# One kernel of full attention and two local-attention layers: step orders rearranged, first weights loaded a phase earlier

## The chip, the cores and the metric

The kernel runs on one core of a Trainium2 chip. The metric is device time in microseconds (us) of one execution. The times of before are three runs; the profile is one further execution of the same program.

## The reference, cut to what matters

The input `x` is 16 sequences of 512 rows and 256 columns, float32. It is layer-normed once (`xn`), and two branches are computed from `xn`: full attention with 16 heads, and two "layers" of local attention with a gated feed-forward.

```python
xn = layernorm(x)
x  = x + attn(xn, w_qkv, w_out) + layers(xn)
def layer(x):                                   # twice, 8 heads of 64, window 128
    h = shift_token(x); q, k, v = split(h @ wqkv)
    q, k = rotary_xpos(l2norm(q) * qs, l2norm(k) * ksc)
    x = x + local_attention(q * 8, k, v) @ wo   # each block of 128 sees itself and the block before
    h = layernorm(shift_token(x)) * lg + lb
    a, g = split(h @ w1 + b1)
    return x + (a * gelu(g)) @ w2 + b2
```

## The kernel before, in words

The program is two phases, one after the other, each a block of five instruction streams: PE (matmuls and transposes), ACT, DVE, POOL and SP (which issues every DMA). A block ends when all five are through and the last stores have landed; only then does the next begin.

**Full attention** (`full_attention_phase`) walks over the 16 sequences. Its last section, "end", is three rounds: B of sequence 14, B of sequence 15, and the tail T of sequence 15. POOL's last step in it comes some 110 us before its end.

**Layers** (`layers_phase`) first loads and converts weights: SP issues loads of `wqkv`, the two rotation tables, the two scales and `wo`; ACT makes the float16 high parts (`wq_h`, `wo_h`), DVE the low parts (`wq_l`, `wo_l`) and scales the tables; POOL makes identity matrices and masks. SP issues the first of these loads after `const_done`, which DVE's clears raise, and after adding 1 to each of the phase's 55 semaphores (`start_credits`). Behind these six loads it issues the first load of the input, `f_xs`, on whose transposes (step A.XT) everything waits.

The two layers are layer 0 and layer 1. Each walks over the 16 sequences in rounds. A round works on four sequences at once: stream A projects queries and keys of sequence i, C does attention of i-1, D the output projection and N the layer norm of i-2, F the feed-forward of i-3. Thirteen rounds of a layer are one loop body; the first three ("first", "second", "third") and the last ("tail") are written out with some streams missing. The dictionary `order` lists, for each engine, the steps of one round in the order in which the engine issues them; an engine never passes a step that waits. The steps that matter here:

- A.XT transposes the input; A.QK,t projects 128 rows to queries and keys: PE L1026, squares on ACT L1212, on DVE L1350 to L1359, and on POOL the add L1540 (`bt_used`). A.RN is a chain of 12 small DVE operations (L1385, L245 to L250) which ends with `rn_ready` (L1387). A.NM,t scales by it on POOL (L1545, 128x1024), A.HI,t makes high parts on ACT (L1222, L1223), A.SQ,t and A.SH,t the low parts on POOL (L1550, L1535).
- C.V projects values (PE L1026, ACT, DVE L1368). C.L1,hp computes scores to find the row maximum (DVE L1392), C.LM hands the maxima on, C.L2,hp computes the scores of two heads again (PE) and their exponentials (ACT L1245), C.PH,hp the float16 high parts (ACT L1253), C.PL,hp the low parts (DVE L1374, two operations of 128x896, both inputs in SBUF), C.PV,hp multiplies by the values (PE L1113 to L1115) and divides (DVE L1403, L1405).
- D.WO,c is the output projection (PE L1133, DVE L1424). N.LN takes the statistics (DVE L1442), N.LR the root (POOL L1530, L1518 to L1523), N.LA applies them (DVE L1456, eight operations, both source and target in SBUF), N.XH transposes the result (PE L1008, ACT L1262, DVE L1462), N.LS adds a bias (POOL L1562).
- F.W1,f and F.W2 are the feed-forward: F.W1,f on PE L1162, ACT L1268, DVE L1472; F.H1,f on ACT (L1274, L1276) and POOL (L1556); F.ZB adds the full attention's result on DVE (L1433, layer 1 only); F.W2,0 to 2 on PE L1133, with an eviction after part 2 (DVE L1483). On DVE and SP the parts 0 and 1 of F.W2 issue nothing.

The results on PE go to four PSUM slots of 128x1024. Which step gets which slot is not written down: `PsumPlan` walks PE's order once and gives each step the slot used longest ago (a slot used by A.QK counts as used 2.5 steps later). A PE step waits until its slot's former user is drained. Each section starts the walk with the slots in the same turn, so in a loop C.V,0 always takes slot p0, C.V,1 p1, C.V,2 p2 and C.V,3 p3.

Of the kernel before, what the change touches and what calls it, by code (L numbers as in the profile page):

```python
# [1684 lines left out]
```

## Time and profile before

| what | value |
|---|---|
| median of 3 runs | 3927.06 us (3926.61 to 3927.91) |
| time of the profiled execution | 3927.97 us |
| its span, first to last instruction | 3926.1 us |
| mean granted TensorE clock | 0.953 |
| busy: PE, PEld, DVE, ACT, POOL | 3360.0, 1960.8, 2846.7, 2352.7, 1511.6 us |

The full attention fills the span up to 1155.1 us; the layers' first transposes start at 1172.25 us. From there on the rounds follow each other at about 81 us each. The page's busy share is an average over both phases; the waits of one round tell more.

### The profile page before, as it was taken

The numbers are of one execution on the slowest core, as the hardware profiler recorded it, in microseconds if no ns is written. First come the engines' busy times: TensorE is split into PE (matmuls) and PEld (weight loads), VectorE is DVE, ScalarE is ACT, GpSimd is POOL, SyncE is SP. The second block draws the span as 40 slices with busy tenths as digits, with TensorE's granted clock in tenths as the row PEclk, the third lists the DMA queues.
The fourth block names the chain that finished last, engine by engine and source line by source line (L and its number), as shares of the span: only waits on it lengthen the run. The fifth ranks groups of instructions, "written<-read, shape, count | busy, mean of one in ns | idle before, by whom it ended". The sixth has DMA issues, their size and how long they took to land.

```text
span 3926.1 us, 77200 instructions
## 1 busy us (share of the span) xinstructions
PE 3360.0 (86%) x29600; PEld 1960.8 (50%) x29600; DVE 2846.7 (73%) x4121; ACT 2352.7 (60%) x2813; POOL 1511.6 (39%) x1171
## 2 busy tenths in 40 slices
PE   2888888888855799998999989878999899998998
...
GB/s 56 49 61 54 60 53 60 52 60 52 51 50 39 15 20 19 27 19 29 19 20 26 25 23 36 30 44 24 25 32 24 35 29 24 32 29 36 24 27 30
DMA packets 149008, 139.11 MB, mean 35 GB/s; under 512 B 11132, under 2 KB 147376, under 8 KB 148912
## 3 DMA queue, kind: packets, MB, share of 16 engines
...
## 4 chain that ended last, share of the span: by engine, by line
PE 35%; DVE 15%; ACT 11%; issue 7%; POOL 1%; DMA 1%; SPq 0%; DVEq 0%; ACTq 0%; POOLq 0%
PE f_p L1026 13%; PE f_p L1162 7%; DVE f_Ph L1374 6%; PE f_p L1133 5%; PE f_p L1052 3%; PE f_p L1043 3%; ACT f_Ph L1253 2%; ACT f_Pl L1245 2%; DVE f_xh L1456 2%; PE f_p L1059 2%; ACT f_hT L1274 1%; DVE f_rt L248 1%; ACT f_gates L1268 1%; DVE f_xT_l L1343 1%; PE f_p L1008 1%
## 5 line engine op out<-in xcount | busy, mean ns | idle before, releaser
L654 DVE TENSOR_REDUCE m_negm<-m_p 128x2 f16<-128x1024 f32 x512 | 608.7, 1222 | 169.2 <-PE m_p L473 167.5
L576 ACT ACTIVATE m_Pr<-m_p 128x1024 f32<-128x1024 f32 x512 | 500.4, 1020 | 164.0 <-PE m_p L492 159.6
L1374 DVE TENSOR_TENSOR f_Ph<-f_Pl,f_Ph 128x896 f16<-128x896 f32 x256 | 377.0, 1514 | 213.3 <-ACT f_Ph L1253 213.3
L1540 POOL TENSOR_TENSOR f_u<-f_u,f_bt 128x1024 f32<-128x1024 f32 x128 | 301.8, 2358 | 465.6 <-DVE f_bt L1359 465.6
L1556 POOL TENSOR_TENSOR f_hT<-f_gates,f_hT 128x512 f16<-128x512 f32 x192 | 234.2, 1223 | 587.9 <-ACT f_gates L1276 587.6
L1268 ACT ACTIVATE f_gates<-f_p,f_bias 128x512 f32<-128x512 f32 x192 | 131.4, 684 | 469.0 <-PE f_p L1162 469.0
L501 PE MATMUL m_o<-m_Pr,m_vm 128*32 128x512 f32 x2048 | 341.6, 646 | 13.0 <-ACT m_Pr L576 13.0
L1026 PE MATMUL f_p<-f_wq_h,f_xT_h 128*128 128x512 f16 x768 | 307.0, 400 | 26.1 <-DVE f_xhT_l L1462 12.7
L1545 POOL TENSOR_TENSOR f_u<-f_u,f_rn 128x1024 f32<-128x1024 f32 x128 | 289.1, 2258 | 74.3 <-DVE f_mark_v L1387 74.3
L1392 DVE TENSOR_REDUCE f_negm<-f_p 128x4 bf16<-128x1024 f32 x256 | 300.8, 1222 | 17.0 <-PE f_p L1059 16.6
L1026 PE MATMUL f_p<-f_wq_l,f_xT_h 128*128 128x512 f16 x768 | 305.3, 398 | 0.0
L1026 PE MATMUL f_p<-f_wq_h,f_xT_l 128*128 128x512 f16 x768 | 303.1, 395 | 0.0
L1550 POOL TENSOR_TENSOR f_qst<-f_u,f_qst 128x512 f16<-128x512 f32 x128 | 179.6, 1403 | 270.8 <-ACT f_khh L1223 270.8
L1245 ACT ACTIVATE f_Pl<-f_p 128x896 f32<-128x896 f32 x256 | 227.4, 915 | 91.9 <-PE f_p L1097 56.9
L1113 PE MATMUL f_p<-f_vl,f_Ph 128*128 128x65 f16 x1792 | 187.4, 197 | 95.4 <-DVE f_Ph L1374 80.9
L1133 PE MATMUL f_p<-f_w_h,f_hT 128*128 128x256 f16 x1536 | 262.8, 273 | 1.6 <-POOL f_hT L1556 1.4
L473 PE MATMUL m_p<-m_KT,m_QT 48*128 48x512 f16 x1024 | 192.4, 399 | 80.7 <-DMA m_KT<-m_lo 31.4
L1472 DVE SCALAR_TENSOR_TENSOR f_gates<-f_p,f_bias,f_gates 128x512 f32<-128x512 f32 x192 | 141.6, 750 | 161.2 <-ACT f_gates L1268 158.4
L1162 PE MATMUL f_p<-f_xhT_h,f_w_h 128*128 128x512 f16 x640 | 245.0, 383 | 2.4 <-DVE f_mark_h L1464 2.4
L492 PE MATMUL m_p<-m_QT,m_KT 49*128 49x512 f16 x1024 | 191.9, 390 | 61.7 <-DVE m_negm L654 35.8
L1162 PE MATMUL f_p<-f_xhT_h,f_w_l 128*128 128x512 f16 x640 | 244.0, 381 | 0.0
L1162 PE MATMUL f_p<-f_xhT_l,f_w_h 128*128 128x512 f16 x640 | 243.8, 381 | 0.0
...
## 6 DMA issues: line engine op xcount, KB each, us to landing
f_xs<-out SPq DMA_DIRECT2D x32, 512.0 KB, 4.4
f_xr<-out SPq DMA_DIRECT2D x32, 512.0 KB, 5.0
out<-f_xb SPq DMA_DIRECT2D x32, 512.0 KB, 3.0
m_xin<-in_L_attn_x SPq DMA_DIRECT2D x16, 512.0 KB, 4.1
out<-m_xn SPq DMA_DIRECT2D x16, 512.0 KB, 3.0
m_QT<-m_hi SPq DMA_DIRECT2D x128, 64.0 KB
m_KT<-m_hi SPq DMA_DIRECT2D x128, 64.0 KB
m_xr<-in_L_attn_x SPq DMA_DIRECT2D x16, 512.0 KB, 4.7
```

The costliest lines, as they stand in the source:

```text
L501: mm = pe.matmul(psum[w.slot("MV", g)][j * VW:(j + 1) * VW, :], vm[I.par][:, kt, g * HG + j, :], Pr[kt % 2][:, j, :], start=(kt == 0), sto ...
L576: act.activation(Pr[kt % 2][:, 2 * u:2 * u + 2, :].rearrange("p h t -> p (h t)"), psum[w.slot("M2", g, kt, u)][:, :], ACT.Exp).then_inc(*w ...
L654: dve.tensor_reduce(negm[:, t, pr // 2, :, pr % 2], psum[w.slot("M1", h, u)][:, :].rearrange("p (a k) -> p a k", a=2), AX.X, ALU.max, nega ...
L1026: mm = pe.matmul(psum[w.slot(key, t)][:, i * INNER:(i + 1) * INNER], a_[:, c, at], b_[:, c, n0:n0 + INNER], start=(c == 0 and k == 0), sto ...
L1133: mm = pe.matmul(psum[w.slot(key)][:, t * D:(t + 1) * D], a_[:, c, t * P:(t + 1) * P], b_[:, c, :], start=(c == 0 and k == 0 and t % 2 == ...
L1162: mm = pe.matmul(psum[w.slot("W1", f)][0:rows(f), g * T:(g + 1) * T], a_[:, c, hidden(g, f)], b_[:, c, :], start=(c == 0 and k == 0), stop ...
L1245: act.activation(Pl[h % 2][:], psum[w.slot("L2", h)][:, 0:NK], ACT.Exp, scale=1 / KBOOST)\
L1374: dve.tensor_tensor(Pp[h % 4][:, 1, :], Pl[h % 2][:], Pp[h % 4][:, 0, :], ALU.subtract).then_inc(*p_lo_ready.up(I))
L1392: dve.tensor_reduce(negm[:, :, h], psum[w.slot("L1", h)][:, :].rearrange("p (n k) -> p n k", n=NT), AX.X, ALU.max, negate=True).then_inc(* ...
L1540: pool.tensor_tensor(u[t][:], u[t][:], bt[:], ALU.add).then_inc(*bt_used.up(I))
L1545: pool.tensor_tensor(u[t][:].rearrange("p (h d) -> p h d", d=DH), u[t][:].rearrange("p (h d) -> p h d", d=DH), rn[:, t, :].unsqueeze(2).to ...
L1556: pool.tensor_tensor(hT_l[0:n, f, :], hp_[f % 3][0:n, :], hT_h[0:n, f, :], ALU.subtract).then_inc(*hl_ready.up(I))
```

## The change

Two things. First, a new class `First` holds the tensors that both phases now share: the layers' weight tensors for queries, keys, values and output, tables, masks, identities and their staging space. Its `load` issues the first layer's six loads on SP in the full attention's last section, in front of the last tail (step "PW"). Its `constants` and `prepare` run on POOL after POOL's last step of the full attention: identities and masks, then, once all six loads have landed, the conversion of both weights and the scaling of the tables, all with POOL's `tensor_tensor`. In the layers phase ACT and DVE skip these steps for layer 0, and SP raises their semaphores by hand (eight `sem_inc`).

Second, the dictionary `order` of the layers is changed on all five engines.

```diff
+        def load(self, sp, q_scale, k_scale):      # class First
+        start(self.st_q, self.wqkv[0].rearrange("(c p) n -> p c n", p=P))
+        start(self.cos_t[:], ...)   # sin_t, qk_scale 0, qk_scale 1
+        start(self.st_o, self.wo[0].rearrange("(c p) n -> p c n", p=P))
+    def prepare(self, pool):
+        done = 0
+        pool.wait_ge(self.loaded, 6 * 16)
+        for src, high, low in ((self.st_q, self.wq_h, self.wq_l), (self.st_o, self.wo_h, self.wo_l)):
+            def factor(n):
+                return self.factors[:, n:n + 1].unsqueeze(2).to_broadcast([P, src.shape[1], src.shape[2]])
+            for dst, a, b, op in ((src, src, factor(4), ALU.mult), (high[:], src, factor(5), ALU.mult), (low[:], src, high[:], ALU.subtract)):
+                pool.tensor_tensor(dst, a, b, op).then_inc(self.steps, 1)
+                done += 1
+                pool.wait_ge(self.steps, done)
+        for i in range(2):
+            pool.tensor_tensor(cos_t[:, :, i, :], cos_t[:, :, i, :], qk_scale[:, i:i + 1, :]..., ALU.mult)
+            for h in range(2):
+                pool.tensor_tensor(sin_t[:, :, i, half], sin_t[:, :, i, half], ..., ALU.mult)
...
                               woven(order, B=a("B_15", 1, lambda i: last), T=a("T_14", 0, lambda i: last - 1)),
+                              {engine: [("PW", a("weights", 0, lambda i: 0))] for engine in ENGINES},
                               woven(order, T=a("T_15", 1, lambda i: last)))),
...
             w.run({"LN": ln, "PQ": pq, "SP": sp_})
+            first.constants(pool)
+            first.prepare(pool)
...
-        "PE": """... A.QK,3 D.WO,0 C.L1,0 D.WO,1 D.WO,2 D.WO,3 C.L1,1 ...
+        "PE": """... A.QK,3 C.L1,0 D.WO,0 D.WO,1 D.WO,2 D.WO,3 C.L1,1 ...
-        "ACT": """... F.H1,1 F.W1,3 C.LM F.H1,2 F.W1,4 F.H1,3 F.W1,5 F.H1,4 F.H1,5 C.L2,0 C.PH,0 ...
+        "ACT": """... F.H1,1 F.W1,3 F.H1,2 C.LM F.W1,4 F.H1,3 F.W1,5 F.H1,4 C.L2,0 F.H1,5 C.PH,0 ...
-        "DVE": """C.V,0 C.V,1 C.V,2 C.V,3 A.XT D.OT,0 D.OT,1 A.QK,0 A.QK,1 A.QK,2 A.QK,3 D.WO,0 D.WO,1 D.WO,2 C.L1,0 D.WO,3 C.L1,1
-               F.W1,0 C.L1,2 F.W1,1 C.L1,3 C.LM F.W1,2 A.RN F.W1,3 F.W1,4 F.W1,5 F.ZB N.LN F.W2,0 C.PL,0 C.PL,1 F.W2,1 F.W2,2 N.LA
-               C.PL,2 C.PV,0 C.PL,3 C.PV,1 N.XH C.PV,2 C.PV,3""",
-        "POOL": """A.QK,0 A.QK,1 A.QK,2 A.QK,3 F.H1,0 F.H1,1 F.H1,2 F.H1,3 F.H1,4 F.H1,5 A.NM,0 N.LR A.SQ,0 A.SH,0 A.NM,1 A.SQ,1 A.SH,1
-               A.NM,2 A.SQ,2 A.SH,2 A.NM,3 A.SQ,3 A.SH,3 N.LS""",
-        "SP": """A.XT N.LX C.XR F.W2,0 F.W2,1 F.W2,2 N.XH""",
+        "DVE": """C.V,0 C.V,1 C.V,2 C.V,3 A.XT D.OT,0 D.OT,1 A.QK,0 A.QK,1 A.QK,2 C.L1,0 A.QK,3 D.WO,0 D.WO,1 D.WO,2 D.WO,3 C.L1,1
+               F.W1,0 C.L1,2 F.W1,1 C.L1,3 F.W1,2 C.LM F.W1,3 N.LN F.W1,4 A.RN F.W1,5 F.ZB F.W2,0 F.W2,1 C.PL,0 C.PL,1 F.W2,2 N.LA
+               C.PL,2 C.PV,0 C.PV,1 C.PL,3 N.XH C.PV,2 C.PV,3""",
+        "POOL": """A.QK,0 A.QK,1 A.QK,2 F.H1,0 F.H1,1 A.QK,3 F.H1,2 F.H1,3 A.NM,0 F.H1,4 F.H1,5 N.LR A.SQ,0 A.SH,0 A.NM,1 A.SQ,1 A.SH,1
+               A.NM,2 A.SQ,2 A.SH,2 A.NM,3 N.LS A.SQ,3 A.SH,3""",
+        "SP": """A.XT F.W2,0 N.LX C.XR F.W2,1 F.W2,2 N.XH""",
...
             def wq(I):                             # SP; ws(I) likewise with wo_loaded
+                if layer == 0:
+                    for signal, n in ((wq_loaded, 16), (tables_loaded, 64), (w_hi, 1), (w_lo, 1), (tables_done, 1)):
+                        sp.sem_inc(*signal.up(I, n))
+                    return
-                sp.wait_ge(const_done, N_CONST)
```

## Rows read from the trace of the kernel before

**Rows 1.** Windows view: us, busy time by engine, granted clock, DMA share, GB/s.
```profile
1155.10:1172.20 17.10, 0.00 (x0) 0.00 (x0) 6.89 (x19) 3.82 (x2) 8.10 (x21) 0.50 0.54 188
3225.50:3306.30 80.80, 73.72 (x735) 49.52 (x734) 62.27 (x98) 53.24 (x66) 40.46 (x30) 1.00 0.10 29
```

**Rows 2.** Timeline, engine PE: first transpose of A.XT, rounds 3 and 15 of layer 1.
```profile
2737.84 0.32 PE L1008 MATMUL f_p<-f_identf,f_xs 128*128 128x128 f32 x1
...
3711.28 0.33 PE L1008 MATMUL f_p<-f_identf,f_xs 128*128 128x128 f32 x1
```

**Rows 3.** Waits of PE in one round, 3225.5 to 3306.3: total, times, longest.
```profile
PE f_p L1113 <- DVE f_Ph L1374: 2.6, 1, 2.6
...
PE f_p L1008 <- DVE f_on L1405: 0.9, 1, 0.9
PE f_p L1026 <- DVE f_xhT_l L1462: 0.6, 1, 0.6
PE f_p L1085 <- DVE f_gates L1472: 0.5, 1, 0.5
```

**Rows 4.** Timeline of the same round, engine DVE: start, length, operation, wait before.
```profile
3264.15 0.19 DVE L1385 TENSOR_SCALAR f_ss<-f_ss 128x64 f32<-128x64 f32 x1
...
3269.07 0.06 DVE L1387 MEMSET f_mark_v<- 1x1 f32 x1
...
3283.01 3.96 DVE L1374 TENSOR_TENSOR f_Ph<-f_Pl,f_Ph 128x896 f16<-128x896 f32 x2 [2.82 <-ACT f_Ph L1253]
...
3288.15 0.34 DVE L1456 TENSOR_SCALAR f_xh<-f_x,f_mv,f_rstd 128x128 f32<-128x128 f32 x1
...
3290.19 2.10 DVE L1374 TENSOR_TENSOR f_Ph<-f_Pl,f_Ph 128x896 f16<-128x896 f32 x2
...
3294.11 3.96 DVE L1374 TENSOR_TENSOR f_Ph<-f_Pl,f_Ph 128x896 f16<-128x896 f32 x2 [0.98 <-ACT f_Ph L1253]
...
3298.96 1.22 DVE L1462 TENSOR_TENSOR f_xhT_l<-f_p,f_xhT_h 128x1024 f16<-128x1024 f32 x1
...
3301.18 0.69 DVE L1405 TENSOR_TENSOR f_on<-f_p,f_rden 128x512 f32<-128x512 f32 x1
```

**Rows 5.** Timeline of the same round, engine ACT.
```profile
3282.03 1.79 ACT L1253 ACTIVATE f_Ph<-f_Pl 128x896 f16<-128x896 f32 x2
```

**Rows 6.** Timeline of the same round, engine POOL.
```profile
3275.83 1.89 POOL L1545 TENSOR_TENSOR f_u<-f_u,f_rn 128x1024 f32<-128x1024 f32 x1
...
3281.04 1.16 POOL L1550 TENSOR_TENSOR f_qst<-f_u,f_qst 128x512 f16<-128x512 f32 x1
...
3283.27 2.76 POOL L1545 TENSOR_TENSOR f_u<-f_u,f_rn 128x1024 f32<-128x1024 f32 x1
```

**Rows 7.** Timeline of layer 0's third round, engine DVE.
```profile
1356.02 3.05 DVE L1374 TENSOR_TENSOR f_Ph<-f_Pl,f_Ph 128x896 f16<-128x896 f32 x2 [2.14 <-ACT f_Ph L1253]
...
1360.09 1.94 DVE L1456 TENSOR_SCALAR f_xh<-f_x1s,f_mv,f_rstd 128x128 f32<-128x128 f32 x1
```

**Rows 8.** Timeline of layer 0's third round, engine POOL.
```profile
1353.01 1.74 POOL L1518 TENSOR_TENSOR f_rstd<-f_var,f_factors 128x4 f32<-128x4 f32 x1
...
1356.10 2.02 POOL L1550 TENSOR_TENSOR f_qst<-f_u,f_qst 128x512 f16<-128x512 f32 x1
```

**Rows 9.** Timeline between the phases, engine POOL.
```profile
1155.14 0.20 POOL L1494 MEMSET f_ident<- 128x128 f16 x1 [111.36 <-POOLq L377]
```

**Rows 10.** Timeline between the phases, the DMA queue of SP.
```profile
1125.71 0.39 SPq L753 DMA_DIRECT2D m_xr<-in_L_attn_x  x1
...
1158.34 0.38 SPq L1573 DMA_DIRECT2D f_u<-in_L_ffn_wqkv  x1
...
1161.12 0.87 SPq L1573 DMA_DIRECT2D f_Ph<-in_L_ffn_wo  x1
```

**Rows 11.** DMA view, 1120 to 1180: KB each, us from issue to landing.
```profile
f_Ph<-in_L_ffn_wo SPq DMA_DIRECT2D x1, 512.0 KB, 9.6
```

**Rows 12.** The page, DMA issues over the whole span.
```profile
f_xs<-out SPq DMA_DIRECT2D x32, 512.0 KB, 4.4
```

More of the change, by code:

```diff
@@ L298, in full_attention_phase @@
+def full_attention_phase(nc, counts, x, w_qkv, w_out, out, attn_res, first, q_scale, k_scale):
     B, T, D = x.shape
@@ L767, in mp @@
                 sp.dma_start(res_v[I.b], res[:]).then_inc(*res_stored.up(I, 16))
-            w.run({"LX": lx, "XR": xr_, "LS": ls, "ST": stack, "MM": mmax, "MP": mp})
+            w.run({"LX": lx, "XR": xr_, "LS": ls, "ST": stack, "MM": mmax, "MP": mp, "PW": lambda I: first.load(sp, q_scale, k_scale)})
             end = Inst("after", 0, None)
@@ L775, in full_attention_phase, with layers_phase @@
     return ph.measured()
-def layers_phase(nc, counts, wqkv, q_scale, k_scale, wo, ln_g, ln_b, w1, b1, w2, b2, out, attn_res):
+def layers_phase(nc, counts, wqkv, q_scale, k_scale, wo, ln_g, ln_b, w1, b1, w2, b2, out, attn_res, first):
     B, T, D = out.shape
@@ L884, in layers_phase @@
         psum = {s: ctx.enter_context(nc.psum_tensor("f_" + s, [P, 1024], F32)) for s in pools["pair"]}
-        wq_h, wq_l = sb("wq_h", [P, NC, 3 * INNER], F16), sb("wq_l", [P, NC, 3 * INNER], F16)
-        wo_h, wo_l = sb("wo_h", [P, NP_, D], F16), sb("wo_l", [P, NP_, D], F16)
+        wq_h, wq_l, wo_h, wo_l, U, Pall = first.wq_h, first.wq_l, first.wo_h, first.wo_l, first.U, first.Pall
+        cos_t, sin_t, qk_scale, factors = first.cos_t, first.sin_t, first.qk_scale, first.factors
+        ident, identb, identf, masks, mask0, sel = first.ident, first.identb, first.identf, first.masks, first.mask0, first.sel
         w1_h, w1_l = sb("w1_h", [P, NC, 2 * HID], F16), sb("w1_l", [P, NC, 2 * HID], F16)
@@ L949, in layers_phase @@
         sp_held = ctx.enter_context(nc.semaphore("f_sp_held"))
[L950 to L951 removed]
+        const_done = ctx.enter_context(nc.semaphore("f_const_done"))
+        N_CONST = 7
         out_v = out.rearrange("b (t p) d -> b p t d", p=P)
@@ L1588, in ws @@
             def ws(I):
-                if I.b > 0:
-                    hold(on_ready.at(all_of_layer(I.b), 0))
+                if I.b == 0:
+                    for signal, n in ((wo_loaded, 16), (w_hi, 1), (w_lo, 1)):
+                        sp.sem_inc(*signal.up(I, n))
+                    return
+                hold(on_ready.at(all_of_layer(I.b), 0))
                 load(I, wo_loaded, st_o, wo[I.b].rearrange("(c p) n -> p c n", p=P))
@@ L1648, in program @@
     attn_res = nc.dram_tensor("attn_res", x.shape, F32, kind="Internal").ap()
-    found = full_attention_phase(nc, counts, x, w_qkv, w_out, out, attn_res)
-    return found | layers_phase(nc, counts, wqkv, q_scale, k_scale, wo, ln_g, ln_b, w1, b1, w2, b2, out, attn_res)
+    with ExitStack() as ctx:
+        first = First(nc, ctx, out, wqkv, wo)
+        found = full_attention_phase(nc, counts, x, w_qkv, w_out, out, attn_res, first, q_scale, k_scale)
+        return found | layers_phase(nc, counts, wqkv, q_scale, k_scale, wo, ln_g, ln_b, w1, b1, w2, b2, out, attn_res, first)
 _INS = ["L0_attn_x", "L0_attn_w_qkv", "L0_attn_w_out", "L0_ffn_wqkv", "L0_ffn_q_scale", "L0_ffn_k_scale", "L0_ffn_wo",
```

118 lines of the change are left out of this document (75 added, 43 removed).

## The prediction

> **What bounds the kernel now.** I read the windows view first: in the 17.1 us between the phases PE does nothing, and in a round of the layers it is busy 73.7 of 80.8 us [rows 1]. The reader is to see two kinds of gain: the gap between the phases, and the 7 us of PE's gaps in each of 26 loop rounds. A.XT comes every 81.1 us ((3711.28 - 2737.84) / 12) [rows 2], so a change of 0.3 us in the round is a change of 8 us, or 0.2% of the kernel; that is also what I take to be indistinguishable from no change.
>
> The waits of PE in a round say where the gaps are [rows 3]: 2.6 us in front of C.PV,3 for DVE's low parts, 0.9 in front of N.XH's transposes, 0.6 in front of C.V,0, 0.5 in front of C.L2,0; a further 1.5 in front of C.L2,3 is a wait for F.W2's slot. All but the 0.5 lie in the last 28 us of the round. There the chain is not PE's: it goes exponentials, C.PH (ACT), C.PL (DVE), C.PV. The timelines of DVE and POOL show what stretches it. A pair of C.PL operations takes 2.10 us alone, but 3.96 in C.PL,1 and C.PL,3 [rows 4], and the A.NM that POOL starts 0.26 us into C.PL,1 takes 2.76 instead of 1.89 [rows 6]. So one waits until the other's operation is over: A.NM for the first of the pair, the second of the pair for A.NM. What matters in that stretch is who comes when, not how much each engine has to do.
>
> **The preload.** Removed between the phases: the wait for the loads and their conversion, up to A.XT. What stays ahead of A.XT is SP's credits, the load of `f_xs` and its landing. The credits alone put SP's first DMA 3.2 us behind the start of the phase (1158.34 - 1155.14) [rows 9, 10]; eight more at 3.2 / 55 add 0.5; landing takes 4.4 [rows 12]. A.XT thus starts 8.3 us into the phase instead of 17.1: -8.8.
>
> Added: the phase now begins only when POOL is through. The loads go out where the tail's `m_xr` load did, at 1125.7 [rows 10]. On the old path the last of them went out 2.8 us after the first and landed 9.6 later [rows 10, 11]; so they land at 1138.1. POOL's identities and masks lie in its 111.36 us of idleness [rows 9] and cost nothing. The conversion: 128x1024 float32 with one operand repeated from one number takes POOL 1.89 us, two operands of 128x512 1.16 [rows 6]. Weights for queries: two multiplications of 3072 columns (5.7 each) and one subtraction (6.9); for the output a third of that; tables six small ones, 2.5 together. Sum 18.3 + 6.1 + 2.5 = 27, end 1165.2. The phase before ended at 1155.1, so +10.1. Net +1.3 us. If every operand cost the two-operand rate (2.3 per 1024 columns), 3 us more; if the loads land 3 us earlier, with no `f_xs` behind them, 3 less: -2 to +4.5.
>
> The Trainium skill (GPSIMD Engine Reference, section 3.1) gives 4497 ns for a two-input float32 operation of 2048 columns, 2.2 us per 1024, without a cheaper rate for a repeated operand; the row with its 1.89 is below it. By the page the conversion would take 29 us and the preload +3.5.
>
> The tail's `m_xr` load moves behind six issues and 7 us of traffic, to about 1140; its reader runs at 1150, so nothing waits. On the path it would cost its lateness.
>
> **Moves at no cost.** C.L1,0 in front of D.WO,0 on PE finds both slots free (those of A.ST,3, which ACT drains in time); DVE then does C.L1,0 in front of A.QK,3, which comes 2.5 us later and still before the eviction of D.WO; 0.3 us of lateness ends in DVE's idle time ahead of F.W1,0. POOL's A.QK,3 behind F.H1,1 fills idle time; its readers are A.NM,3 and nobody sooner. N.LS in front of A.SQ,3 delays A.ST,3 of the next round, 13 us away. The parts of F.W2 moved on SP and DVE issue nothing. Without these covers each is worth under 1 us a round.
>
> **Gains in the round.** A.RN leaves the place in front of F.W1,3's eviction, which frees C.L2,0's slot: -0.5, the whole wait [rows 3]. C.L2,0's exponentials go ahead of F.H1,5. C.PV,1 goes ahead of C.PL,3 into DVE's idle 0.98 [rows 4], so N.XH's eviction no longer stands behind it: -0.9. These would make the round 1.4 us shorter if C.PL,3 ended as early as before.
>
> **Losses.** First, A.RN. It ran from 3264.15 to 3269.07 [rows 4], with two stalls. Behind F.W1,4 it starts at 3269.6 and, with one stall of 1, ends at 3273.5. POOL meanwhile has nothing (F.H1,4 now stands behind A.NM,0). Then A.NM,0, F.H1,4 and F.H1,5 take 1.9 + 1.16 + 1.16 and end at 3277.8, just when A.NM,0, then the last of the three, ended before (3275.83 + 1.89) [rows 6]. But C.PL,0 is ready at 3276.9, 1.2 earlier than before, and queues ahead of N.LR. Layer 0's third round has this order already: N.LR's second operation takes 1.74 us there, and A.SQ,0 starts only at the moment of C.PL,1 [rows 7, 8]. In the new round N.LR so ends at 3282.2 instead of 3281.0, C.PL,1 is ready at 3282.4 (C.PH's first operation, 3282.03 before [rows 5], half a us earlier), and A.SQ,0 and A.SH,0 push in: C.PL,1 ends at 3285.4 to 3286.5 (3286.97 before), but A.NM,1 has not run yet. It starts at 3286.5 where it had ended at 3286.0, just in front of N.LA. N.LA's operations take 0.34 us and met nobody [rows 4]; in the third round one of them waits 1.94 behind A.NM,1 [rows 7]. So N.LA ends at 3290.4, as before, in spite of the early start; C.PL,2 follows, A.SQ,1, A.SH,1 and A.NM,2 fall between C.PL,2 and C.PL,3, and C.PL,3 ends at 3298.5 against 3298.07: +0.4 where -0.9 was there to be had. In layer 1, F.ZB (128x1024, 1.2 us) waits for A.NM,0 and keeps F.H1,4 waiting; POOL is 1.2 to 1.5 us later, and C.PL,3 ends at 3299.2: +1.1.
>
> Of this the rule is the Trainium skill's (SBUF, State Buffer, section on the two separate sides): a DVE operation with two SBUF inputs or in a two-port mode and a GpSimd operation exclude each other for the whole operation, and whoever starts first goes first. The stretched rows agree. By the rule every C.PL and N.LA operation moved into POOL's busy stretch pays; it speaks against this change.
>
> Second, the slots. Walked, the new PE order gives C.V,0's slot p0 to C.PV,3 (before: to N.XH). C.V,0 now waits for DVE's last C.PV eviction, 2.9 us after C.PL,3 (3298.96 to 3301.87) [rows 4], where it waited only for N.XH's. The order on DVE being N.XH, C.PV,2, C.PV,3, the next A.XT comes 8.45 us after C.PL,3 ends; before it came 8.23 after in layer 1 and 7.75 in layer 0, where no load of `f_xs` is waited for. That is +0.2 and +0.7, and it already holds the gain from moving C.PV,1.
>
> Sum: layer 0 13 x (0.4 + 0.7) = 14, layer 1 13 x (1.1 + 0.2) = 17. The third rounds get A.RN behind N.LN: +1.5 each; the two tails, with no stream A, keep the gains: -1.5 each. With the preload +1.3 the profiled execution's 3927.97 becomes 3960; it lies 0.9 above the median, so 3959 to 3960.
>
> **Rivals.**
> 1. As computed: +0.5 to +1.9 a round, 3940 to 3980. For it speaks that the third round shows each collision. 0.46.
> 2. Faster: A.NM,1 gets in ahead of N.LA and C.PL,3's two operations run back to back, which takes 2.10 instead of 3.96 [rows 4]. C.PV,1 ahead of C.PL,3 makes this possible: if C.PL,3 starts after the second C.PH has ended, its second operation queues ahead of A.NM,2. Then C.PL,3 ends at 3296.2, -1.9, with the slots -1.4 a round, -37 in all: 3890. It decides whether A.NM,2 is issued before or after C.PL,3's second operation is ready, a matter of 0.5 us. Against it: N.LR's and A.SQ,0's lateness. 0.23.
> 3. Even: only one collision goes away, and slots and preload take it back: 3920 to 3935. 0.17.
> 4. F.H1,5 comes later than the 3280 at which F.W2,2 needs it, and PE's chain slips as well: +2.5 a round, 3992. 0.14.
> That the preload fails to take effect is no rival of its own: it is worth under 5 us either way.
>
> Range: 3888 to 3985; the likeliest case alone 3940 to 3980. Faster 0.24, same 0.19, slower 0.57.
>
> **What would show it.** A.XT first at 1173 to 1175, POOL busy up to 1165. Loop rounds of 82.2 (layer 0) and 82.4 (layer 1). No wait of PE ahead of C.L2,0; C.V,0 waiting for L1405; N.LA's L1456 with operations of 1 to 2 us in every round; A.NM,1 starting behind 3286 in a round that starts at 3225.5. If L1456 stays at 0.34 and C.PL,3 lasts 2.1, the second case holds. If C.V,0 still waits for L1462, I walked the slots wrongly.

## The result, and the profile after

The changed kernel takes 3987.9 us (median of 4 runs, 3982.1 to 3990.2) against 3926.8 for the kernel before: ratio 1.0154, 95% interval 1.0138 to 1.0170, 61 us slower. The prediction was 3960 with a range to 3985: the direction was right, the loss of 61 us nearly twice the 33 computed, and 3 us beyond the range's end. The profiled execution took 3986.68 us with a span of 3984.9, 58.8 more than before. PE was busy 3396.1 us against 3360.0 for the same 29600 matmuls, and its mean granted clock was 0.939 against 0.953. That is a first hint: part of the loss is that the same work ran more slowly.

Cut at the starts of A.XT, the 58.8 us are: -4.3 up to the first A.XT; +0.4 in layer 0's three written-out rounds; +10.7 in twelve loop rounds (81.07 to 81.96 each); +1.6 in the stretch between the layers (layer 0's last loop round and its tail); +7.5 in layer 1's three written-out rounds; +28.5 in twelve rounds of layer 1 (81.12 to 83.49); +14.4 from there to the end (the last loop round, the tail and the last stores).

Timeline of the changed kernel, engine PE: the A.XT of rounds 3 and 15 of layer 1 (the answer to [rows 2]). Line numbers of `layers_phase` have shifted: by 77 on PE, by 80 to 84 on ACT and DVE, by 63 on POOL. In e1, e3 and e4 below they are 7 lower than in the changed kernel.
```profile
2753.77 0.31 PE L1085 MATMUL f_p<-w_identf,f_xs 128*128 128x128 f32 x1
...
3755.68 0.49 PE L1085 MATMUL f_p<-w_identf,f_xs 128*128 128x128 f32 x3
```
Windows view of the changed kernel: two consecutive rounds of layer 1, then the last 16 and 19 us of each (columns as in [rows 1]).
```profile
3257.00:3339.10 82.10, 74.74 (x736) 51.11 (x735) 63.32 (x97) 53.03 (x65) 42.64 (x29) 0.98 0.10 29
3339.10:3424.20 85.10, 78.38 (x735) 53.07 (x734) 64.73 (x99) 53.33 (x65) 45.28 (x32) 0.92 0.09 28
3323.00:3339.10 16.10, 10.49 (x121) 7.33 (x118) 11.77 (x19) 9.35 (x13) 14.13 (x8) 0.89 0.21 65
3405.00:3424.20 19.20, 14.38 (x128) 9.51 (x124) 12.82 (x21) 9.88 (x13) 15.44 (x9) 0.64 0.16 55
```
The two rounds differ by 3.0 us. In their last stretch the granted clock is 0.89 in the one and 0.64 in the other, while C.PL,3 ends at 74.1 us of the round in both. Most rounds of layer 1 alternate between these two kinds. So a round has to be read in two parts: up to the end of C.PL,3, which the chain of DVE, ACT and POOL sets, and from there to the next A.XT, where the last evictions and PE's own matmuls set the pace, at whatever clock PE is granted.

Waits of PE in the first of these rounds (the answer to [rows 3]): total, times, longest.
```profile
PE f_p L1085 <- DVE f_on L1489: 3.1, 1, 3.1
PE f_p L1103 <- DVE f_on L1489: 1.3, 1, 1.3
PE f_p L1190 <- DVE w_Ph L1458: 1.2, 1, 1.2
PE f_p L1210 <- POOL f_hT L1619: 1.1, 1, 1.1
PE f_p L1200 <- DVE f_xT_l L1427: 0.4, 1, 0.4
PE f_p L1210 <- DVE f_gates L1556: 0.3, 1, 0.3
```
N.XH (L1085) waits 3.1 us for the eviction of C.PV,0, whose slot it gets; C.V,0 (L1103) waits 1.3 for that of C.PV,3; C.PV,3 (L1190) waits 1.2 for C.PL,3; F.W2,2 waits 1.1 for F.H1. The wait ahead of C.L2,0 that the change removes is indeed gone.

Timeline of that round, engine DVE (the answer to [rows 4]).
```profile
3300.79 0.29 DVE L1526 BATCH_NORM_STATS2 f_stats<-f_x 128x6 f32<-128x128 f32 x1 [2.46 <-DMA f_x1s<-f_x]
...
3303.42 0.18 DVE L1469 TENSOR_SCALAR f_ss<-f_ss 128x64 f32<-128x64 f32 x1
...
3306.46 0.06 DVE L1471 MEMSET f_mark_v<- 1x1 f32 x1
...
3309.91 3.60 DVE L1458 TENSOR_TENSOR w_Ph<-f_Pl,w_Ph 128x896 f16<-128x896 f32 x2 [0.33 <-ACT w_Ph L1333]
...
3315.33 2.11 DVE L1458 TENSOR_TENSOR w_Ph<-f_Pl,w_Ph 128x896 f16<-128x896 f32 x2 [1.82 <-ACT w_Ph L1333]
...
3318.61 1.20 DVE L1540 TENSOR_SCALAR f_xh<-f_x,f_mv,f_rstd 128x128 f32<-128x128 f32 x1
3319.73 1.94 DVE L1540 TENSOR_SCALAR f_xh<-f_x1s,f_mv,f_rstd 128x128 f32<-128x128 f32 x1
...
3323.14 2.08 DVE L1458 TENSOR_TENSOR w_Ph<-f_Pl,w_Ph 128x896 f16<-128x896 f32 x2
...
3327.04 3.97 DVE L1458 TENSOR_TENSOR w_Ph<-f_Pl,w_Ph 128x896 f16<-128x896 f32 x2
```
Same round, engine POOL (the answer to [rows 6]).
```profile
3306.60 1.90 POOL L1608 TENSOR_TENSOR w_u<-w_u,f_rn 128x1024 f32<-128x1024 f32 x1 [3.83 <-DVE f_mark_v L1471]
3308.46 4.10 POOL L1619 TENSOR_TENSOR f_hT<-f_gates,f_hT 128x512 f16<-128x512 f32 x2
...
3318.58 1.15 POOL L1598 TENSOR_TENSOR f_klt<-w_u,f_khh 128x512 f16<-128x512 f32 x1
3319.69 1.90 POOL L1608 TENSOR_TENSOR w_u<-w_u,f_rn 128x1024 f32<-128x1024 f32 x1
```
The first row of DVE is what the prediction left out: N.LN, moved ahead of F.W1,4, waits 2.46 us for the transfer of shifted rows `f_x1s`, and A.RN (L1469 to L1471) with `rn_ready` stands behind it. Relative to its round's start A.RN ends at 49.5 us, not at 48.0 as computed and not at 43.6 as before. Further down most collisions are where they were computed: N.LA's first two operations take 1.20 behind A.SH,0 and 1.94 against A.NM,1, C.PL,1 its short 2.11, C.PL,3 still 3.97. Not computed was that F.H1,4 and 5 take 4.10 where they meet F.ZB and C.PL,0, and that C.PL,0 takes 3.60. C.PL,3 ends at 74.0 (72.6 before), 1.4 late; +1.1 was computed.

The preload: conversion on POOL, from landing to the last table.
```profile
1133.27 5.31 POOL L366 TENSOR_TENSOR w_u<-w_u,w_factors 128x3072 f32<-128x3072 f32 x1 [85.01 <-DMA w_Ph<-in_L_ffn_wo]
...
1158.42 0.86 POOL L375 TENSOR_TENSOR w_sin<-w_sin,w_qk_scale 128x128 f32<-128x128 f32 x2
```
It takes 26.0 us (27 computed). The first A.XT comes at 1168.0; in the other profiles of kernels with the preload, below, it comes anywhere from 1167.3 to 1174.2, so its -4.3 here is within the scatter of single executions. In e1's profile the loads land at 1138.0, where they were computed, and the first A.XT comes at 1172.9.

### The profile page after: what moved, and what is told of

Its sections match the earlier page's. It is cut to its first block, busy times and chain, and to the rows that moved or that the text cites. A ratio compares the mean times of both kernels' runs of the same rounds, so it can differ in the third digit from the quotient of the medians.

```text
span 3984.9 us, 77447 instructions
## 1 busy us (share of the span) xinstructions
PE 3396.1 (85%) x29600; PEld 2002.9 (50%) x29600; DVE 2847.3 (71%) x4115; ACT 2349.6 (59%) x2811; POOL 1596.6 (40%) x1185
## 4 chain that ended last, share of the span: by engine, by line
PE 22%; DVE 17%; DMA 11%; issue 9%; ACT 8%; POOL 2%; SPq 1%; DVEq 0%; POOLq 0%; ACTq 0%
PE f_p L1103 12%; DMA f_x1s<-f_x 11%; DVE w_Ph L1458 4%; PE f_p L1120 2%; DVE f_xh L1540 2%; ACT w_Ph L1333 2%; ACT f_Pl L1325 2%; DVE f_negm L1476 1%; PE f_p L1239 1%; PE f_p L1210 1%; DVE f_ss L1434 1%; PE f_p L1129 1%; DVE f_xT_l L1427 1%; ACT f_hT L1354 1%; DVE w_u L1437 1%
## 5 line engine op out<-in xcount | busy, mean ns | idle before, releaser
L1603 POOL TENSOR_TENSOR w_u<-w_u,f_bt 128x1024 f32<-128x1024 f32 x128 | 302.3, 2361 | 492.2 <-DVE f_bt L1443 492.2
L1619 POOL TENSOR_TENSOR f_hT<-f_gates,f_hT 128x512 f16<-128x512 f32 x192 | 250.7, 1312 | 595.4 <-ACT f_gates L1356 595.4
L1458 DVE TENSOR_TENSOR w_Ph<-f_Pl,w_Ph 128x896 f16<-128x896 f32 x256 | 364.3, 1462 | 120.1 <-ACT w_Ph L1333 119.0
L1103 PE MATMUL f_p<-w_wq_h,f_xT_h 128*128 128x512 f16 x768 | 306.7, 399 | 43.9 <-DVE f_on L1489 32.0
L1608 POOL TENSOR_TENSOR w_u<-w_u,f_rn 128x1024 f32<-128x1024 f32 x128 | 270.1, 2110 | 184.5 <-DVE f_mark_v L1471 184.5
L1476 DVE TENSOR_REDUCE f_negm<-f_p 128x4 bf16<-128x1024 f32 x256 | 301.3, 1224 | 28.8 <-PE f_p L1136 28.5
L1103 PE MATMUL f_p<-w_wq_l,f_xT_h 128*128 128x512 f16 x768 | 303.5, 395 | 0.0
L1103 PE MATMUL f_p<-w_wq_h,f_xT_l 128*128 128x512 f16 x768 | 302.2, 394 | 0.0
L1190 PE MATMUL f_p<-f_vl,w_Ph 128*128 128x65 f16 x1792 | 208.4, 206 | 64.9 <-DVE w_Ph L1458 45.2
L1613 POOL TENSOR_TENSOR f_qst<-w_u,f_qst 128x512 f16<-128x512 f32 x128 | 209.0, 1633 | 132.4 <-ACT f_khh L1303 132.4
```

The lines of the kernel that those rows point to most:

```text
L1103: mm = pe.matmul(psum[w.slot(key, t)][:, i * INNER:(i + 1) * INNER], a_[:, c, at], b_[:, c, n0:n0 + INNER], start=(c == 0 and k == 0), sto ...
L1458: dve.tensor_tensor(Pp[h % 4][:, 1, :], Pl[h % 2][:], Pp[h % 4][:, 0, :], ALU.subtract).then_inc(*p_lo_ready.up(I))
L1476: dve.tensor_reduce(negm[:, :, h], psum[w.slot("L1", h)][:, :].rearrange("p (n k) -> p n k", n=NT), AX.X, ALU.max, negate=True).then_inc(* ...
L1603: pool.tensor_tensor(u[t][:], u[t][:], bt[:], ALU.add).then_inc(*bt_used.up(I))
L1608: pool.tensor_tensor(u[t][:].rearrange("p (h d) -> p h d", d=DH), u[t][:].rearrange("p (h d) -> p h d", d=DH), rn[:, t, :].unsqueeze(2).to ...
L1619: pool.tensor_tensor(hT_l[0:n, f, :], hp_[f % 3][0:n, :], hT_h[0:n, f, :], ALU.subtract).then_inc(*hl_ready.up(I))
```

## The experiments

For each kernel two numbers were read from its trace, as means over twelve loop rounds of each layer: when C.PL,3 ends in its round (start and length of the last L1458 row), and how long it takes from there to the next A.XT. "Base" is the changed kernel with the five orders of before. Times are medians; the kernel before ran beside them at 3927.6 to 3928.4.

| kernel | us | C.PL,3 ends, layer 0 / 1 | then to A.XT, layer 0 / 1 |
|---|---|---|---|
| before | 3928 | 72.6 / 72.6 | 8.5 / 8.5 |
| changed | 3987.9 | 73.3 / 74.1 | 8.7 / 9.4 |
| e1 preload alone (base) | 3925.1 | 72.6 / 72.6 | 8.5 / 8.5 |
| e2 orders alone | 3970.9 | 72.6 / 73.5 | 9.3 / 9.1 |
| e3 changed, N.LN back | 3947.5 | 71.9 / 72.5 | 10.3 / 9.4 |
| e11 changed, N.LN and C.L1,0 back | 3901.5 | 72.0 / 72.6 | 8.0 / 8.0 |
| e13 changed, C.L1,0 back | 3954.3 | 73.2 / 74.0 | 8.1 / 7.9 |
| e14 base, C.L1,0 moved | 3996.4 | 72.6 / 72.6 | 11.0 / 11.1 |
| e6 e3, C.L1,0 back on PE alone | 3958.0 | 74.0 / 75.2 | 8.1 / 7.8 |
| e10 e3, C.PV,0 early | 3996.7 | 72.6 / 72.8 | 10.9 / 10.9 |
| e5 e3, A.RN back | 4039.9 | 74.7 / 74.6 | 10.8 / 10.7 |
| e12 e5, A.QK,3 back | 3964.8 | 72.6 / 72.6 | 10.1 / 10.1 |
| e4 changed, A.NM,0 back | 4062.1 | 75.3 / 75.3 | 10.1 / 10.4 |
| e8 base, C.L2,0 and A.RN moved | 3988.3 | 75.2 / 75.2 | 7.9 / 8.4 |
| e7 base, C.PV,1 early | 3910.2 | 72.6 / 72.6 | 8.0 / 8.0 |
| e9 e7, A.NM,1 held | 3878.2 | 71.4 / 71.5 | 7.9 / 7.9 |

**Halves of the change.** e1 keeps the preload and has all orders of before; e2 is the kernel before with the new orders.

> The changed kernel with all five orders of before: the preload alone. Theory: the preload costs what the account of the phase boundary gives (8.8 us of gap gone, some 10 us of POOL conversion added), so 3928 us against 3926.9. Rival: the 5.6 us by which the full attention was shorter in the profile of after come with the preload, then 3922. If the preload were part of the loss, it would be above 3935.

> The kernel before with the five new orders and no preload. Theory: the orders are the whole loss: 3983 to 3990 us. Rival: orders and preload interact (the weights of both phases lie elsewhere in SBUF), then under 3975.

e1: 3925.1, ratio 0.9991 (0.9982 to 1.0000): the preload is worth between nothing and 7 us, 3 by the medians. e2: 3970.9, ratio 1.0107 (1.0092 to 1.0123), under both figures of its theory and on its rival's side: the halves don't add up (+43 and -3 against +61). The loss is the orders', but they cost 63 us on top of the preload (3987.9 against e1's 3925.1) and 43 without it. The rows show where some of it comes from: the second of the two issues that fill `f_x1s` (the shifted rows that N.LN waits for) takes 11.4 us on SP's queue (median) in the kernel before and in e2, and 11.8 in e1 and in the changed kernel, and N.LN's wait in a loop round is 1.8 to 2.0 us in e2 and 2.4 to 2.7 in the changed kernel. Loop rounds of layer 1 with the short last stretch are 81.5 and 82.1. So the slower transfer goes with the preload, which puts tensors elsewhere, and not with the orders; why it does stays open.

**N.LN.**
```diff
-  DVE  ... C.LM F.W1,3 N.LN F.W1,4 A.RN F.W1,5 F.ZB F.W2,0 ...
+  DVE  ... C.LM F.W1,3 F.W1,4 A.RN F.W1,5 F.ZB N.LN F.W2,0 ...      # e3
```


> The changed kernel with one step of DVE moved: N.LN stands behind F.ZB again, as before, and not ahead of F.W1,4. Theory A: the step that fails in the prediction is N.LN's wait of 2.6 us for the DMA f_x1s, which delays A.RN, F.H1,4 and 5 and all behind; without it each of 26 rounds gets 1.5 to 2.5 us back: 3922 to 3950. Theory B (the prediction's own: A.RN's new place, the collisions behind it and the slots): N.LN is only a fraction, 0 to 0.5 us a round: 3973 to 3988.

3947.5, ratio 1.0049 (1.0036 to 1.0063): 40 us came back, inside theory A's range. C.PL,3 ends 1.5 us earlier in layer 1 and 1.3 in layer 0; A.RN ends at 48.0 instead of 49.5, just where the prediction had put it. But C.PL,3 now ends at 71.9 and 72.5, ahead of the kernel before, where the prediction without any wait had it at 73.0 and 73.7: the rest of its chain was 1.1 to 1.2 us too slow. In layer 0 of e3 N.LA's operations take 0.67 us at the most, not 1.94. Much of the written-out rounds' loss goes as well: layer 1's first round falls from 75.6 to 67.5 us (65.4 before), the stretch behind the last A.XT of the loop from 229.2 to 214.3. Yet the second part of the round grows, in layer 0 from 8.7 to 10.3 us. N.LN's wait is one cause, and there is another.

The transfer in the chain of the changed kernel's round (start, length, what) with a window of 10 us in it, then the wait for it in layer 1's first round, where N.LN comes early for want of other work, in the kernel before and in the changed one.
```profile
3284.76 16.00 DMA f_x1s<-f_x
```
```profile
3286.00:3296.00 10.00, 10.00 (x66) 5.12 (x65) 6.89 (x8) 4.22 (x7) 1.15 (x1) 1.00 0.08 19
```
```profile
DVE f_stats L1442 <- DMA f_x1s<-f_x: 2.5, 1, 2.5
```
```profile
DVE f_stats L1526 <- DMA f_x1s<-f_x: 8.6, 1, 8.6
```
`f_x1s` is half of x1's columns, each row moved one partition on, so the copy writes 127 partitions (254 KB) in a first issue and the rows that wrap around (1.5 KB) in a second. It lands 16.0 us after the second issue. While it is the only transfer, the DMA share is 0.08 of 16 engines, the time of little more than one, and 19 GB/s move; `f_xs`, twice the size, lands in 4.3 us. So the rows show a copy that is hardly spread over the engines; whether one that is spread would end N.LN's wait was not tried. In the chain of the whole changed kernel the transfer holds 11% of the span.

**The slots: C.L1,0.** By a walk over PE's order, moving C.L1,0 ahead of D.WO,0 gives C.V,0 the slot of C.PV,3. Three kernels put it back (e6 on PE alone), and one moves it alone.
```diff
   PE   ... A.QK,3 [C.L1,0] D.WO,0 [C.L1,0] D.WO,1 ...      # first place: change, second: before
   DVE  ... A.QK,2 [C.L1,0] A.QK,3 D.WO,0 D.WO,1 D.WO,2 [C.L1,0] D.WO,3 ...
   # e6:  e3, PE alone back      e11: e3, PE and DVE back
   # e13: changed kernel, both back      e14: base, both moved
```


> N.LN behind F.ZB as in the run before, and on PE C.L1,0 behind D.WO,0 again, which by the walk of the slots gives C.V,0 back the slot of N.XH. Theory (the prediction's slot step): 0.2 us a round in layer 1 and 0.7 in layer 0, so 8 to 14 us below N.LN alone (3947): 3933 to 3939. Rival: C.V,0's wait only moves to another step of the same stretch, since all evictions there stand behind C.PL,3: 3943 to 3950.

3958.0, ratio 1.0073 (1.0056 to 1.0090), slower than e3 by 11 us, which neither side expected. Waits of PE in a round of e6:
```profile
PE f_p L1085 <- DVE f_on L1489: 3.1, 1, 3.1
PE f_p L1129 <- DVE f_bt L1443: 1.9, 1, 1.9
```
With DVE still in the new order, C.L1 (L1129) waits 1.9 us in mid-round for A.QK,2's slot, and C.PL,3 comes 2.1 to 2.7 us later than in e3. Behind C.PL,3 the run does show what C.V,0's slot is worth: no wait of C.V,0 is left, and the second part of the round falls from 10.3 and 9.4 to 8.1 and 7.8 us.

> The changed kernel with N.LN behind F.ZB (3947), and C.L1,0 back on both engines: on PE behind D.WO,0, on DVE behind D.WO,2. In the run with PE's C.L1,0 alone back, PE waited 1.9 us for the drain of A.QK,2's slot. Theory: that wait is gone, and C.V,0 has N.XH's slot, which gives 0.3 us a round: 3932 to 3942. Rival: C.L1,0's place does not matter: 3944 to 3950.

3901.5, ratio 0.9931 (0.9914 to 0.9947): 46 us below e3 and faster than the kernel before. Three times the most that the theory gave. C.PL,3 ends where it does in e3; all of the gain lies behind it. The fastest kind of round of layer 0 in e11, then e3's slowest, cut 70 us after their starts (windows view; the means over layer 0 are 79.9 and 82.2).
```profile
1779.10:1849.10 70.00, 66.68 (x669) 45.99 (x667) 55.33 (x88) 48.21 (x58) 34.25 (x26) 1.00 0.09 26
1849.10:1858.78 9.68, 6.87 (x66) 3.53 (x67) 5.49 (x10) 4.42 (x7) 7.99 (x6) 1.00 0.00 0
```
```profile
1705.67:1775.67 70.00, 66.65 (x669) 46.03 (x667) 54.72 (x87) 48.20 (x58) 32.99 (x24) 1.00 0.09 26
1775.67:1789.39 13.72, 10.64 (x66) 5.51 (x67) 6.67 (x11) 4.91 (x7) 9.63 (x7) 0.63 0.00 0
```
The same 66 matmuls take PE 6.87 us in the one and 10.64 in the other. The granted clock is 1.00 (2.4 GHz) against 0.63, a mixture with the lower level of 1.2 GHz. In both rounds PE stood 1.3 us ahead of N.XH and 2.6 ahead of C.PV,3; in e3 it stood another 1.0 ahead of C.V,0, and the projections of C.V that follow ran at half clock, where nothing but PE sets the pace. The Trainium skill says that frequent short idle stretches between groups of matmuls make the clock swing between its two levels (TensorE: Matmul & The Clock Gate, the section on PSUM-queue cycling). These two rounds agree. Which of several rounds with the same waits is hit, the rows do not show.

> The changed kernel (3988) with C.L1,0 alone back, on PE behind D.WO,0 and on DVE behind D.WO,2; N.LN stays ahead of F.W1,4. Theory: C.V,0's wait for C.PV,3's eviction is a second gap near the end of the round, and with it PE's clock falls to half for longer; without it 1.0 to 1.8 us a round come back, beside N.LN's wait which stays: 3938 to 3962. Rival: the two share one cause, and with N.LN's wait in place C.L1,0 is worth little: 3975 to 3990.

> Preload and the five orders of before (3925), with C.L1,0 alone moved as in the change: on PE ahead of D.WO,0, on DVE ahead of A.QK,3. Theory: C.V,0 gets the slot of C.PV,3, whose eviction comes last, and PE's clock stays low longer: 1.2 to 2 us a round, 3955 to 3977. Rival: the prediction's slot step, 0.2 to 0.7 us a round: 3930 to 3940.

e13: 3954.3, ratio 1.0069 (1.0052 to 1.0086), 34 us back with N.LN's wait in place, as its theory has it. e14: 3996.4, ratio 1.0176 (1.0159 to 1.0193): this one move in the old orders costs 71 us over e1, more than the whole change, and more than its theory gave. Windows of a round of e14 and of one of e1, from 70 to 83 us behind their starts at 3185.24 and 3144.03, each followed by the timeline row of the first matmul of C.V,0.
```profile
3255.24:3268.24 13.00, 9.16 (x71) 5.04 (x68) 8.07 (x14) 5.30 (x8) 9.63 (x7) 0.74 0.24 81
```
```profile
3261.69 0.61 PE L1103 MATMUL f_p<-w_wq_h,f_xT_h 128*128 128x512 f16 x1 [1.25 <-DVE f_on L1489]
```
```profile
3214.03:3227.03 13.00, 9.79 (x87) 5.52 (x85) 8.81 (x15) 5.99 (x10) 9.63 (x7) 0.87 0.25 81
```
```profile
3218.77 0.61 PE L1096 MATMUL f_p<-w_wq_h,f_xT_h 128*128 128x512 f16 x1 [0.64 <-DVE f_xhT_l L1539]
```
C.V,0 starts at 76.45 in its round instead of 74.74: +1.7, the direct cost of the slot in the old DVE order. A loop round is 2.5 longer than in e1; the other 0.8 goes with the clock. In e1 it is 1.00 in rounds of 80.3 to 81.1 us and 0.98 in those of 80.6 to 81.6; in e14 it is 0.96 in every loop round, and no round is under 82.9.

**A.RN, A.QK,3 and the order on POOL.** e5 takes e3 and puts A.RN back ahead of F.W1,3; e12 takes e5 and puts POOL's A.QK,3 back behind A.QK,2; e4 takes the changed kernel and puts A.NM,0 behind F.H1,5; e8 takes base, puts A.RN behind F.W1,3 and, on ACT, C.L2,0 ahead of F.H1,5.

> The changed kernel with two steps of DVE back where they were: N.LN behind F.ZB, and A.RN ahead of F.W1,3. Theory: with N.LN alone back, rn_ready still comes 4.4 us later than before; with A.RN back too, A.NM,0 and F.H1,4 start earlier and only C.V,0's slot and the 3.1 us gap ahead of N.XH are left: 3925 to 3940. Rival: A.RN's place is indifferent once N.LN has gone, or its new place is even good (C.L2,0's slot comes free sooner): 3945 to 3955.

> The kernel of 4040 (N.LN and A.RN back on DVE) with POOL's A.QK,3 back behind A.QK,2. Theory: in the 4040 kernel A.QK,3 of 2.4 us on POOL ran into A.RN, one of whose operations took 2.3 us and two 1.1, and rn_ready came 2 us late; with A.QK,3 back this goes away: 3915 to 3935. Rival: the 4040 comes from F.H1,4 and F.H1,5 or the clock alone: above 4000.

e5: 4039.9, ratio 1.0284 (1.0267 to 1.0301), far above both figures. DVE and then POOL in a round of it:
```profile
3345.60 2.29 DVE L249 SCALAR_TENSOR_TENSOR f_rt<-f_rt,f_ss 128x64 f32<-128x64 f32 x1
```
```profile
3345.45 2.36 POOL L1603 TENSOR_TENSOR w_u<-w_u,f_bt 128x1024 f32<-128x1024 f32 x1
```
An operation of 0.23 us on DVE takes 2.29 because A.QK,3's addition on POOL has begun 0.15 us ahead of it; A.RN ends 2.0 us late, and F.W1,3's eviction behind it frees C.L2,0's slot 2.0 us later than before (PE stands 2.6 us there). e12 removes that: 3964.8, ratio 1.0098 (1.0081 to 1.0115), 75 us better, but not the 3915 to 3935 of its theory. What is left of it looks like C.V,0's slot again, though no run takes that out of e12: its C.PL,3 ends at 72.6, as in the kernel before, and PE waits 1.0 to 1.3 ahead of C.V,0; its rounds of layer 1 take 82.0 to 82.2 at a clock of 0.98 and 83.1 to 83.7 at 0.96.

> The changed kernel with one step of POOL moved: A.NM,0 behind F.H1,5 again, as before, and not ahead of F.H1,4. Theory C: F.H1,4 and F.H1,5 behind A.NM,0 are what holds PE in layer 1 (1.1 us in each loop round) and in the written-out rounds (11 and 5 us): 3950 to 3965. Theory B: POOL's order is indifferent, since A.RN's lateness moves everything anyway: 3983 to 3992.

> Preload and the orders of before, with the two moves that aim at C.L2,0: on DVE A.RN behind F.W1,3, on ACT C.L2,0 ahead of F.H1,5. Theory: C.L2,0 starts 0.5 us earlier on PE and 1.3 us earlier on ACT, A.RN ends 1.4 us later, and C.PL,1 follows C.PH,1, whose row showed PE's F.W2 as the next limit: -0.5 to +0.5 us a round, 3912 to 3938. Rival: F.H1,5's lateness makes PE wait ahead of F.W2,2: above 3945.

e4: 4062.1, ratio 1.0338 (1.0324 to 1.0353); e8: 3988.3, ratio 1.0150 (1.0133 to 1.0167). e4 was expected at or below what it started from. e8's time is on its rival's side, but not by the rival's path: PE does not wait for POOL ahead of F.W2,2. POOL and then ACT in a round of e8 that starts at 3268.23, and POOL in a round of e4 that starts at 3318.65:
```profile
3320.73 1.15 POOL L1619 TENSOR_TENSOR f_hT<-f_gates,f_hT 42x512 f16<-42x512 f32 x1 [2.68 <-ACT f_gates L1356]
3321.84 1.89 POOL L1608 TENSOR_TENSOR w_u<-w_u,f_rn 128x1024 f32<-128x1024 f32 x1
```
```profile
3323.77 0.63 ACT L1302 ACTIVATE f_qst<-w_u 128x512 f16<-128x512 f32 x1 [1.44 <-POOL w_u L1608]
```
```profile
3371.23 1.15 POOL L1612 TENSOR_TENSOR f_hT<-f_gates,f_hT 42x512 f16<-42x512 f32 x1 [3.42 <-ACT f_gates L1349]
3372.34 1.90 POOL L1601 TENSOR_TENSOR w_u<-w_u,f_rn 128x1024 f32<-128x1024 f32 x1
```
ACT's F.H1,5 now comes behind the exponentials of C.L2,0; POOL waits 2.68 us for it (3.42 in e4), and A.NM,0 stands behind. A.HI,0 on ACT waits for A.NM,0, and C.L2,1's exponentials stand behind A.HI,0. In both kernels A.NM,0 starts 53.6 or 53.7 us into the round, against 49.6 in the changed one, and C.PL,3 ends at 75.2 to 75.3. So C.L2,0 ahead of F.H1,5 (ACT) needs A.NM,0 ahead of F.H1,4 (POOL): without it the move cost 63 us in the old orders (e8, in which A.RN was moved too) and 74 in the new ones (e4). POOL's move without ACT's was not run.

**The gap ahead of N.XH.**
```diff
-  DVE  ... N.LA C.PL,2 C.PV,0 C.PV,1 C.PL,3 ...      # e3
+  DVE  ... N.LA C.PV,0 C.PL,2 C.PV,1 C.PL,3 ...      # e10
```


> The changed kernel with N.LN behind F.ZB (3947) and, on DVE, C.PV,0 ahead of C.PL,2. N.XH's slot is that of C.PV,0, so the 3.1 us in which PE stands ahead of N.XH should shrink to under 1. Theory: behind that gap PE's clock falls to half, which costs 1.4 to 2.4 us in three of four rounds; without the gap the rounds go to 80.6: 3908 to 3925. Rival: the idle time moves to C.PV,3 and the clock falls as often: 3940 to 3950.

3996.7, ratio 1.0177 (1.0160 to 1.0194): the rival's path, and a time far above it. Waits of PE in a round of e10, then DVE in the round behind it:
```profile
PE f_p L1190 <- DVE w_Ph L1458: 3.6, 2, 2.2
PE f_p L1085 <- DVE f_on L1489: 1.1, 1, 1.1
PE f_p L1103 <- DVE f_on L1489: 1.0, 1, 1.0
```
```profile
3341.07 3.36 DVE L1458 TENSOR_TENSOR w_Ph<-f_Pl,w_Ph 128x896 f16<-128x896 f32 x2
...
3346.25 2.09 DVE L1458 TENSOR_TENSOR w_Ph<-f_Pl,w_Ph 128x896 f16<-128x896 f32 x2 [0.86 <-ACT w_Ph L1333]
```
The 3.1 us ahead of N.XH shrank to 1.1, but C.PL,2 came later and the idle time moved ahead of C.PV,2 and C.PV,3. C.PL,2 takes 3.36 us, and C.PL,3, in every loop round, only 2.1: its two operations run back to back, which the prediction had as its second rival. It starts so much later that it ends where it did, so nothing was gained. The mean granted clock fell to 0.923, the lowest of all runs, and the second part of the round took 10.9 us. It is not the length of the one gap that decides.

**Two pieces that gain.** e7 is base with C.PV,1 ahead of C.PL,3 on DVE, as in the change. e9 is e7 and has POOL's A.NM,1 wait until C.PL,1 is done.
```diff
             pool.wait_ge(*rn_ready.at(I, 1))
+            if t == 1 and not (isinstance(I.b, int) and I.b == 0):
+                pool.wait_ge(p_lo_ready.sem, (I.b - 1) * p_lo_ready.per + 5)      # e9
```


> Preload and the five orders of before (3925 alone), with one step of DVE moved: C.PV,1 ahead of C.PL,3, as in the changed kernel. Theory: the eviction falls into DVE's idle 0.98 us, N.XH's slot does not depend on it, and C.PL,3's second operation is still parted from the first by POOL; worth -0.9 to +0.3 us a round: 3902 to 3933. Rival (case 2 of the prediction): the two operations of C.PL,3 run back to back, 1.9 us a round: 3875 to 3895.

> Preload, orders of before and C.PV,1 ahead of C.PL,3 (3910 without what follows), and POOL's A.NM,1 now waits until C.PL,1's second operation is done. Theory: an operation of DVE with all operands in SBUF and one of POOL exclude each other, so C.PL,1 falls from 3.96 to 2.1 us; the next limits (A.HI,1 and C.L2,3 on ACT) leave 0.3 to 0.7 us a round of it: 3891 to 3903. Rival: C.PL,1's second operation is late for another reason (its input), then C.PL,1 stays at 3.9 and A.NM,1 is 2 us later: 3910 to 3945.

e7: 3910.2, ratio 0.9952 (0.9935 to 0.9968), 15 us under e1: 0.5 to 0.6 us a round, all of it behind C.PL,3 (8.5 to 8.0). C.PL,3 still takes 3.97 us, so the back-to-back case did not occur here. e9: 3878.2, ratio 0.9874 (0.9857 to 0.9890), the fastest of all, 49 us under the kernel before. DVE and then POOL in one of its rounds:
```profile
3167.70 2.24 DVE L1458 TENSOR_TENSOR w_Ph<-f_Pl,w_Ph 128x896 f16<-128x896 f32 x2 [2.83 <-ACT w_Ph L1333]
...
3171.12 0.89 DVE L1540 TENSOR_SCALAR f_xh<-f_x,f_mv,f_rstd 128x128 f32<-128x128 f32 x1
```
```profile
3170.02 1.90 POOL L1610 TENSOR_TENSOR w_u<-w_u,f_rn 128x1024 f32<-128x1024 f32 x1 [2.03 <-DVE w_Ph L1458]
```
C.PL,1 falls from 3.95 to 2.24 us by nothing but A.NM,1's later start, and N.LA pays 0.55 of it. C.PL,3 ends 1.1 us earlier, against the 0.3 to 0.7 expected. That the two engines' operations exclude each other is thereby shown by moving one of them.

## Why the prediction was right in sign and short in size

**Where the 27 us lie.** The profiles differ by 58.8 us, the prediction computed 32 for them. By its own terms, computed and measured: up to C.PL,3, 20 and 28 us; behind C.PL,3, 12 and 15; the written-out rounds, nothing and 21; the preload, +1.3 and -4.3. So 21 of the 27 missing us lie in the written-out rounds.

**The step that failed: N.LN's wait, put at nothing.** "Behind F.W1,4 it starts at 3269.6" has N.LN ahead of A.RN with its old durations and no wait. `f_x1s` lands 16 us after its second issue, 2.5 us after DVE is there. e3 prices the whole of it at 40 us (it moves N.LN's 2 us of work too, which in the changed order would fit into 2.06 us of DVE's idle time ahead of F.W1,4): C.PL,3 ends 1.3 to 1.5 us earlier in each loop round (in layer 0 the second part of the round takes that back), 15 us come from behind the last A.XT of the loop, 8 from layer 1's first round. There N.LN waits 8.6 us and PE 11.1 for F.H1,4:
```profile
PE f_p L1210 <- POOL f_hT L1619: 11.1, 1, 11.1
```
"The third rounds get A.RN behind N.LN: +1.5 each" was near (+1.9 and +1.8). What it left out is the first round of layer 1, 65.4 to 75.6, of which the second gave 4.5 back, and the tail, which was to gain and in layer 1 lost some 12 us: there little other work lies between A.RN and its readers.

**The loop rounds up to C.PL,3: near by luck.** The sums were +0.4 in layer 0 and +1.1 in layer 1; measured +0.7 and +1.5. But e3, in which N.LN does not wait, has -0.7 and -0.1. So the missed wait (+1.3 and +1.5) and a chain computed 1.1 to 1.2 too slow nearly cancelled. Where that chain is too slow is seen only in part: in e3's layer 0 N.LA does not meet A.NM,1 for long, where the prediction had 1.94.

**The slots: right in place, near in the sum, wrong in what they are worth.** The walk was right: C.V,0 waits for L1489. "That is +0.2 and +0.7" came out as +0.9 in layer 1 and +0.2 in layer 0, together 1.1 for 0.9, and this too is luck. The base was misread: 8.23 and 7.75 for the kernel before are single rounds at a clock of 1.00, while its loop means are 8.5 in both layers, since most of its rounds have 0.98. And 8.45 was too much for a round that the clock spares there: 8.07 in e3, against 7.75 in e11 with the slot undone. By the prediction's rows the move of C.L1,0 is then worth 8.45 - 7.75, 0.7 us a round or 18 in all; measured it is 34 us (e13), 46 on top of e3, and 71 in the old orders (e14, where 1.7 us a round are C.V,0's later start). What the sum had no term for is PE's clock: in the changed kernel's layer 1 the mean of 9.4 hides rounds of 8.1 and of 11.0 us.

**How the two make 61.** Undone alone they give back 40 and 34 us, together 86, so each costs some 12 us more once the other is gone: the price of a wait depends on the other waits near it. The 26 us that e11 lies under the kernel before can be e7's 15, e1's 3 and 8 of what else the orders bring; no run takes those 8 apart.

**The preload.** +1.3 computed, -3.3 measured in e1 (-7 to 0 by its interval): as good as nothing. In e1's profile each part lies within 1 us of where it was computed, and the first A.XT comes at 1172.9 for 1173.5. In the changed kernel's own profile the loads went out 5.7 us earlier than computed, since the full attention was that much ahead in that execution.

**Moves at no cost.** True only in their company. A.QK,3 behind F.H1,1 on POOL cost 75 us where A.RN has not moved out of its way (e5 against e12); where it has, the rows show no DVE operation stretched by it, and no run prices it. C.L1,0 was called free here by its own wait; its cost was counted under the slots.

**Gains.** C.PV,1 ahead of C.PL,3: -0.9 computed, -0.5 to -0.6 measured (e7). C.L2,0's wait is gone. **Rivals.** The unsplit C.PL,3 never came in the changed kernel; in e10 it came and gained nothing. The fourth has the nearest time, 3992, but not the mechanism: PE's wait for F.H1 is 1.1 us in a loop round of layer 1, not 2.5, and there is none in layer 0.

**Open.** Why the clock falls in one round and not in the next of equal waits, why `f_x1s` holds SP's queue 0.4 us longer with the preload, where the prediction's chain was too slow in layer 1, and a version that joins e9 with e11's gains, which was not tried.
